# Ten products of zeros per batch, added to TensorE's queue in the attention layers of a graph network

## The reference

```python
q = (x @ qw + qb).reshape(N, HEADS, CH)
k = (x @ kw + kb).reshape(N, HEADS, CH)
v = (x @ vw + vb).reshape(N, HEADS, CH)
alpha = jnp.sum(q[dst] * k[src], axis=-1) * SCALE
m = jax.ops.segment_max(alpha, dst, num_segments=N)
a = jnp.exp(alpha - m[dst])
...
msg = v[src] * a[:, :, None]
out = jax.ops.segment_sum(msg, dst, num_segments=N)
```

## Time and profile before

| | us |
|---|---|
| median of 3 runs (7315.26 to 7345.11) | 7339.02 |
| the profiled execution | 7387.36 |
| its span, first to last instruction | 7385.6 |

### The profile page before, as it was taken

How to read it: one execution, slowest core, us unless ns; L and a number is a source line. 1 busy time by engine, 2 the same in 40 slices (tenths; PEclk the granted TensorE clock), 3 DMA queues, 4 the chain that set the end, 5 groups by cost and what they waited for, 6 DMA issues and landing times. The chain is left out here.

```text
span 7385.6 us, 52462 instructions
## 1 busy us (share of the span) xinstructions
PE 3472.8 (47%) x13958; PEld 2190.6 (30%) x13961; DVE 4041.8 (55%) x5328; ACT 1570.5 (21%) x3310; POOL 4192.4 (57%) x4238
## 2 busy tenths in 40 slices
PE   5566555664565565585233334323333423333465
PEld 3445444553454454442111111101111111111133
DVE  5556565664565665675444544434545334445488
ACT  1111111111111111102222222222222222222233
POOL 2555556535655565434766764766665576666321
PEclk7566666675666666686565566555556655556677
DMA  3455555535555555464222322322232222233242
GB/s 99 134 154 152 151 153 156 152 90 145 156 155 155 150 159 149 114 243 127 90 87 86 100 87 81 95 81 91 91 96 89 78 90 87 89 93 96 65 180 98
DMA packets 542142, 876.27 MB, mean 119 GB/s; under 512 B 85127, under 2 KB 383600, under 8 KB 533931
## 3 DMA queue, kind: packets, MB, share of 16 engines
q0 software_dynamic: 167776, 479.21, 21.8%
q1 hardware_dynamic: 373698, 392.93, 17.1%
q10 hardware_dynamic: 390, 0.77, 0.0%
HBM read 552.11 MB, written 320.46 MB: 118 GB/s over the span
## 5 line engine op out<-in xcount | busy, mean ns | idle before, releaser
L1376 POOL DMA_INDIRECT big<-h_tab,big x2352 | 2250.1, 957 | 1136.8 <-issue 822.1
L597 POOL DMA_INDIRECT big<-kv_tab,big x1664 | 1630.9, 980 | 1217.5 <-DVE big L807 680.9
L1422 PE MATMUL psum<-big 128*128 128x512 f32 x1176 | 1059.5, 1054 | 2256.7 <-ACT big L1399 1342.9
L1459 DVE TENSOR_TENSOR psum<-psum,big 128x1024 f32<-128x1024 f32 x294 | 554.5, 1886 | 1766.0 <-remote 1227.0
L1422 PEld LDWEIGHTS psum<-big 128*128 128x128 f32 x1176 | 333.4, 313 | 2822.1 <-ACT big L1399 1482.2
L1393 ACT COPY big<-big 128x1024 f32<-128x1024 f32 x294 | 565.9, 1925 | 2519.6 <-DVE big L1442 2182.2
L724 PE MATMUL psum<-big 128*128 128x128 bf16 x1408 | 568.6, 404 | 971.6 <-issue 500.8
L768 PE MATMUL psum<-big 128*128 128x136 f32 x3328 | 792.2, 398 | 185.1 <-DVE big L838 91.5
L678 ACT COPY big<-psum 125x128 f32<-125x128 f32 x1408 | 376.5, 267 | 2074.7 <-PE psum L724 871.7
L768 PEld LDWEIGHTS psum<-big 128*128 128x128 f32 x3328 | 682.2, 287 | 246.6 <-issue 204.4
L802 DVE TENSOR_TENSOR big<-psum,big 128x512 f32<-128x512 f32 x416 | 286.7, 689 | 825.1 <-remote 616.3
(11 more groups left out here) (405 smaller groups left out, 3376.8 us busy)
## 6 DMA issues: line engine op xcount, KB each, us to landing
run_tab<-big SPq DMA_DIRECT2D x294, 512.0 KB
snap_tab<-big SPq DMA_DIRECT2D x176, 448.0 KB
item_tab<-big SPq DMA_DIRECT2D x208, 272.0 KB
big<-loc_tab SPq DMA_DIRECT2D x104, 512.0 KB
big<-h_tab,big POOLq DMA_INDIRECT x2352
big<-kv_tab,big POOLq DMA_INDIRECT x1664
snap_tab<-big SPq DMA_DIRECT2D x176, 52.0 KB
kv_tab<-big SPq DMA_DIRECT2D x12, 512.0 KB, 2.6
```

The source lines that it names most:

```text
L597: nc.gpsimd.indirect_dma_start(out=kv_ring[:, b % SLOTS, k, :], out_offset=None, in_=kv_tab, in_offset=bass.IndirectOffsetOnAxis(ap=src_it ...
L1376: nc.gpsimd.indirect_dma_start(out=got[j % RING][:, k * D:(k + 1) * D], out_offset=None, in_=h_tab, in_offset=bass.IndirectOffsetOnAxis(ap ...
L1422: ins_ = nc.tensor.matmul(bank[2 * (j % DEEP) + k][:, :], ea_T[j % DEEP], w_blocks[:, k * 512:(k + 1) * 512], start=True, stop=True)
L1459: nc.vector.tensor_tensor(by_feature(msg[j % DEEP]), by_feature(msg[j % DEEP]), got[j % RING].rearrange("p (t f) -> p f t", f=D), ALU.add) ...
```

## The change

A small tile of zeros in bfloat16, cleared once at the start by GpSimd, is multiplied by itself: each product has 128 rows of weights and 512 moving columns (the same 128 columns read four times) and writes bank 6 of PSUM, which nothing reads. Five such products are put in PE's queue ahead of the L768 products of every turn, and five behind them; they wait for nothing and set no semaphore.

```diff
+        zeros = sb("zeros", P, BF)
...
+        def keep_warm(out, count):
+            for _ in range(count):
+                nc.tensor.matmul(out.rearrange("p (k n) -> p k n", n=P), zeros[:, :], zeros[:, :].unsqueeze(1).to_broadcast([P, 4, P]), start=True, stop=True)
...
+                    link_(nc.gpsimd.memset(zeros[:, :], 0.0))
...
                             for n in turn[2:3]:
                                 tally(n)
+                            keep_warm(bank[6][:, :], 5)
                             b = t - BEHIND
                             if b >= 0:
                                 pe.wait_ge(va_done, b + 1)
...
                             elif turn[3:]:
                                 tally(turn[3])
+                            keep_warm(bank[6][:, :], 5)
                             if t % 2 == 0 and t + 2 < BATCHES:
                                 at = windows_of(t + 2)
```

## The result

The changed kernel takes 7595.22 us (median of 3 runs, 7589.23 to 7611.27) against 7339.02: a ratio of 1.037, 95% interval 1.035 to 1.040, or 256 us more. The sign was as forecast, the size was not: 465 us had been worked out.

A forecast was written before the change was run, and what follows sets the result against it. The prediction took a tally, copy, tally chain through PE's program order as the bound. Uncovered products 1.85, less clock 0.42 and held copies 0.3, gave 1.1 us a batch, 465 us over 416 batches: 7800 us, range 7200 to 8300.

The forecast's parts named there:

- The products' price: Ten 512-column products in PE's queue cost 0.265 us each at clock 0.88, 2.65 us a turn.
- The idle time taken: PE's idle time at the products' places and earlier completions: 0.8 us covered plus 0.3 us given back a batch.
- 0.8 us of cover: PE idle time ahead of L768 and the next turn's first tally hides 0.8 us of products; bounds nothing and 2.1.
- 0.3 us of held copies given back: ScalarE's late copies shrink from 2.24 to 1.9 us a batch as gathers fill less of a longer batch.
- The clock's credit: A higher PE clock shortens only the L768 products on the chain, saving 0.42 us a batch.
- hidden at either level: PE's `ask` products fit behind the tally-copy hand-over at low or high clock, so no clock credit was counted.
- The 1.36 us: Skill rule's credit, half of PE's low-clock busy time a batch, set against 0.42; also the clock-alone rival, 6775 us, chance 0.05.
- The chain: Tally, ScalarE's copy, next tally, through PE's program order with L768 once a turn, sets the pace; 6.62 us a batch.
- The rival with sooner completions: A denser PE queue keeps completions prompt, halving 2.24 us of held copies a batch: 7150 us, chance 0.20.
- the sign: ScalarE's "remote" idle time falling by a third or more a batch would show sooner completions and the forecast wrong.
- The products did not hide: Rival: PE's 2.6 us of idle time a batch absorbs the products, time stays at 7340 us; chance 0.12.
- the clock did not stay low: Rival: PE's clock stays low, products paid at 0.43 us each, 8200 us towards 8800; chance 0.13.

The follow-up runs named there:

- the narrow products: The changed kernel with its ten products a turn at 128 columns instead of 512; 7496 us, ratio 1.022 to the kernel before.
- the twenty: The changed kernel with twenty products of 512 columns a turn instead of ten; 7899 us, ratio 1.078 to the kernel before.
- the two banks: The kernel before, with tallies alternating between PSUM banks 7 and 6, each waiting for the copy before last; 7377 us, ratio 1.006.
- the pauses: The kernel before, with GpSimd clearing a small tile between gathers: one after each 7129 us, two after every second 7251, one after every second 7319.

## Why the prediction was right in sign and too high in size

**The products' price was right.** Said: 2.65 us a turn at a clock of 0.88. The trace: starts 0.256 us apart in the groups, 2.56 us a turn, at 0.87. PE was to be busy for near 0.8 (0.787), and L768's mean to fall towards 300 ns (314).

**The idle time taken was right in sum, by luck.** Said: 0.8 us of cover and 0.3 us of held copies given back, 1.1. PE's idle time fell from (1,000 - 603)/151.1 = 2.63 to (1,000 - 787)/139.1 = 1.53 us a batch, by 1.10. Neither part came as said. That it is the idle time at the place of the products that covers them is not borne out: either half alone cost the same. And of held completions more came back than 0.3 us: 1.09 at VectorE, 0.42 at ScalarE.

**The clock's credit was the term mis-sized.** The step "On the chain a higher clock shortens one thing: the L768 products" gave 0.42 us. PE's busy time less the products went from 3.99 to 5.66 - 2.56 = 3.10 us a batch: 0.89 us given back. The L768 products alone gave 294.3/151.1 - 192.2/139.1 = 0.57, and `ask`, which I had called hidden at either level, 225.7/151.1 - 160.6/139.1 = 0.34 (these rows overlap others a little). 2.56 - 1.10 - 0.89 = 0.57, the measured lengthening; with 0.42 it would have been 1.04. Busy and idle time of PE make up a batch whatever the cause, so this sum says which term was off, not what sets the pace.

The Trainium skill's rule that I had set against this term ("TensorE: Matmul & The Clock Gate", section Terms: the throttled time times the share of pulses taken away) was misapplied there. The 1.36 us takes all of the time at the low level away, while the forecast itself took it only from 68% to 24%. By the rule that makes half of 4.0 x 0.44, an estimate of 0.88 us, and half of 3.99 x 0.42 = 0.84 with the clock as measured, 0.66 to 0.87. The trace agrees: 0.89. For the narrow products the rule gives 0.36 and the rows 0.41, for the twenty 1.32 and 1.16. With that estimate of 0.88 for 0.42 the sum of the prediction would have been 0.67 us a batch, 279 us, where 256 were measured. The tallies still take 0.40 us at either level, as I had said against it (0.397 now).

**The chain was read one link too short.** "So the chain is: tally, copy, tally, through PE in its program order" fell with the two banks. What costs most in the kernel before is VectorE's wait for completions that long series of gathers hold, 2.12 of 6.62 us a batch: spacing the gathers takes these waits away and shortens the kernel, as the pauses show. So `ask`, on whose end VectorE's L802 waits, counts as much as the L768 products. That this is why its 0.34 us came back on the path is argued from these rows, not shown by a run.

**The rival with sooner completions was half right.** It wanted half of the held time gone; VectorE's held waits fell by just that, 2.12 to 1.03 us a batch, though ScalarE's, which I named as the sign, only from 2.24 to 253.0/139.1 = 1.82. But it took the products' cost as 0.67 us, and PE's own work now makes VectorE wait for 1.60 us more. Nor does the denser queue seem to be what brought them sooner. A slower turn spaces the gathers, to 5.8 in a series instead of 7.6; with the pauses, the clock as low as before (0.68) and the products absent, they come sooner still.

The products did not hide and the clock did not stay low. In the kernel with half of the gathers, where no held completions could be given back and PE had less idle time, they cost 493 us.

## What to carry to other kernels

Before pricing work that is put into one engine's queue, read what each other engine waits for, the rows without a named releaser too: a chain that is tight need not be the one that sets the pace, and loosening it in a trial costs one run. Filler products raised the clock as they were meant to, and each version of them cost more than the clock gave back. Where a producer issues in bursts and the consumer stalls in answer, slowing the producer a little can be worth trying: 11% on the usual step of the gathers took 2.7% off the kernel, two other ways of pausing 1%.

## What the runs showed of the hardware that was not expected

While gathers follow each other every 1.25 us, the semaphores of TensorE's products reach ScalarE and VectorE late, by 2.74 us in the mean for ScalarE's copies after 7 to 12 us of an unbroken series, although the rows show the products ended; in the kernel with half of the gathers copies followed tallies after 0.04 to 0.07 us in the mean throughout the series of two. A break of 0.14 us after each gather brings the 7 to 12 us row down to 0.51 us in the mean, though about three quarters of the some 100 copies past 12 us are still late, by 1.75 us in the mean over all of them; the same break after every second gather leaves the 7 to 12 us row at 2.36. What in the chip holds the completions stays open, and so does whether the break counts by its length or by what GpSimd does in it. The Trainium skill says that for such transfers a core of GpSimd computes the descriptors itself ("DMA: Bandwidth & Descriptors", section SWDGE vs HWDGE vs iDMA), and no run here shows whether that work or its writes are in the way of them.
